# Gate and up projection on bare 4-bit values: two matmul passes, a PSUM bank for each scale group, scales applied as the banks are read

## The reference

```
h = layernorm(x) * (1 + ca) + sa;   x = x + ga * attention(h, W_Q, W_K, W_V, W_O)     # causal
h = layernorm(x) * (1 + cb) + sb;   x = x + gb * ffn(h)

ffn(x):
    w_gu   = LUT[nibbles of gate_up_packed] * gate_up_scales     # [2816, 512], 4 groups of 128 inputs
    w_down = LUT[nibbles of down_packed] * down_scales           # [512, 1408]
    gate, up = split(x @ w_gu.T)                                 # 1408 features each
    y = (silu(gate) * up) @ w_down.T
    return y / sqrt(mean(y * y) + 1e-6)
LUT = 0, 0.5, 1, 1.5, 2, 3, 4, 6 and their negatives
```

## Time and profile before

| | |
|---|---|
| median of 3 runs | 2338.56 us (2337.83 to 2340.6) |
| the profiled execution | 2341.84 us |
| span of its trace | 2339.8 us |
| TensorE matmul busy | 2235.7 us, 96% of the span |
| Vector engine, ScalarE, GpSimd busy | 52%, 42%, 27% |
| mean granted TensorE clock | 0.982 of full speed |

### The profile page before, as it was taken

One profiled execution on the slowest core, in us unless ns is written; L12 is line 12 of the kernel. 1 busy time (PEld: TensorE's weight loads), 2 busy tenths in 40 slices (PEclk: granted clock), 3 DMA queues, 4 the chain that ended last, 5 costly groups with the idle time before them and its releaser, 6 DMA issues. The chain is left out here.

```text
span 2339.8 us, 38212 instructions
## 1 busy us (share of the span) xinstructions
PE 2235.7 (96%) x12912; PEld 1909.9 (82%) x12912; DVE 1218.2 (52%) x2846; ACT 975.6 (42%) x1852; POOL 632.7 (27%) x470
## 2 busy tenths in 40 slices
PE   5899999999999999999999999999958888999899
PEld 3788888888888888888888888888847676888787
DVE  7364655656565565656555464555635553111465
ACT  4354544545455454545545454555523322111211
POOL 3435262543526254352601011010333330000000
PEclk8999999999999999999999999999979999999999
DMA  5111111101111110111100000000157763000121
GB/s 193 39 46 35 35 34 41 51 23 45 34 34 34 43 49 23 45 34 34 34 30 24 14 20 11 25 9 26 37 177 227 215 215 108 18 27 27 37 67 63
DMA packets 102320, 133.32 MB, mean 57 GB/s; under 512 B 9984, under 2 KB 68224, under 8 KB 102272
## 3 DMA queue, kind: packets, MB, share of 16 engines
q1 hardware_dynamic: 84128, 120.62, 16.2%
q10 hardware_dynamic: 18144, 12.06, 1.6%
HBM read 90.83 MB, written 33.95 MB: 53 GB/s over the span
## 5 line engine op out<-in xcount | busy, mean ns | idle before, releaser
L963 DVE TENSOR_SCALAR_CACHE_REDUCE probs<-ps_s 128x512 f32<-128x512 f32 (+3 forms) x640 | 371.2, 607 | 263.2 <-PE ps_t L830 116.8
L974 DVE TENSOR_TENSOR pT_lo<-ps_t,pT_hi 128x512 fp32r<-128x512 f32 (+3 forms) x640 | 368.6, 605 | 242.8 <-ACT pT_hi L895 241.6
L895 ACT ACTIVATE pT_hi<-ps_t 128x512 fp32r<-128x512 f32 (+3 forms) x640 | 318.7, 531 | 230.4 <-PE ps_t L830 229.6
L906 ACT ACTIVATE probs<-probs,rmin 128x128 f32<-128x128 f32 (+15 forms) x256 | 308.1, 1203 | 150.1 <-DVE rmin L967 124.9
L190 PE MATMUL ps_z<-pT_hi,v_hi 128*128 128x256 f32 (+1 forms) x1152 | 333.7, 290 | 0.3 <-issue 0.3
L190 PE MATMUL ps_p<-hT_hi,w_hi 128*128 128x512 f32 x768 | 320.7, 418 | 8.3 <-POOL halves L708 3.7
L191 PE MATMUL ps_z<-pT_lo,v_hi 128*128 128x256 f32 (+1 forms) x1152 | 324.8, 282 | 0.0
L192 PE MATMUL ps_z<-pT_hi,v_lo 128*128 128x256 f32 (+1 forms) x1152 | 324.7, 282 | 0.0
L830 PE MATMUL ps_t<-ident,probs 128*128 128x128 f32 x2176 | 309.6, 273 | 8.3 <-ACT probs L906 5.8
L192 PE MATMUL ps_p<-hT_hi,w_lo 128*128 128x512 f32 x768 | 303.5, 395 | 0.0
L191 PE MATMUL ps_p<-hT_lo,w_hi 128*128 128x512 f32 x768 | 301.6, 393 | 0.0
(11 more groups left out here) (146 smaller groups left out, 3685.7 us busy)
## 6 DMA issues: line engine op xcount, KB each, us to landing
scratch_zT<-z SPq DMA_DIRECT2D x256, 64.0 KB, 1.6
o_z<-scratch_zT SPq DMA_DIRECT2D x32, 512.0 KB, 4.6
o_scales<-scratch_recips SPq DMA_DIRECT2D x32, 512.0 KB, 5.7
w_raw<-in_w_qkv SPq DMA_DIRECT2D x16, 768.0 KB, 4.7
p_wmod<-in_w_mod SPq DMA_DIRECT2D x6, 1024.0 KB, 10.9
words<-in_gu_packed SPq DMA_DIRECT2D x44, 128.0 KB, 3.4
scratch_wgu<-deq_a SPq DMA_DIRECT2D x22, 256.0 KB, 2.0
g_wraw<-scratch_wgu SPq DMA_DIRECT2D x11, 512.0 KB, 3.5
```

What stands on the lines that cost most here:

```text
L895: nc.scalar.activation(pT[0][:, slot, i % 2, 0:w], ps_t[:, (chunks_before(i) + u) % 2, 0:w], ACT.Copy).then_inc(t_hi, 1)
L906: nc.scalar.activation(probs[:, i % 2, 0:w], probs[:, i % 2, 0:w], ACT.Exp, bias=rmin[:, i % 2:i % 2 + 1], scale=-1.0, accum_out=sums[:, i ...
L963: nc.vector.tensor_scalar(probs[:, i % 2, c * BT:c * BT + w], ps_s[:, at % NB, 0:w], 1.0, None, ALU.mult, ALU.min, accum_out=least).then_i ...
L974: nc.vector.tensor_tensor(pT[1][:, slot, i % 2, 0:w], ps_t[:, (chunks_before(i) + u) % 2, 0:w], pT[0][:, slot, i % 2, 0:w].bitcast(F32), A ...
```

## The change

The gate and up weights are no longer multiplied by their scales in the decoding, and no longer split. The scratch tensor `wgu` holds the bare 4-bit values as fp32r numbers. `gate_up` multiplies them by the high and by the low part of the activations, two passes. Since the scale is different for each chunk of 128 inputs, each of the four chunks gets a PSUM bank of its own. A step is one feature tile, one block of 512 tokens, and gate or up: 88 steps `j` with four banks each, on two sets of banks in turn. The banks are combined with the scale as a number for each partition:

- ScalarE reads banks 0 and 2 and multiplies by their scales (`first_of_pair`, new line 1344);
- the Vector engine reads banks 1 and 3, multiplies by their scales and adds ScalarE's result (`second_of_pair`, 1370), which gives two pairs;
- GpSimd adds the two pairs into `whole` (1396);
- ScalarE applies silu to the gate's `whole` (1352), and the Vector engine multiplies it by the up's `whole` into `mid` (`product`, 1379). Both read SBUF now.

The loops over the feature tiles are written out, without a loop instruction. SyncE loads the codes of tiles 0 and 1 in the output projection, and those of tile n once tile n-2 is done. The scales, 88 rows of 128, are loaded once, widened by ScalarE, transposed by TensorE and copied to SBUF in the output projection's tiles 1 and 2. `decode_piece` has eight instructions for a gate and up piece, one of them on a single column, and nine for a down piece; before it had nine. The 22 loads of gate and up scales in attention are gone.

```diff
 class GateUpWeights(NamedTuple):
-    raw: object
-    parts: object
+    codes: object
+    scales: object
     loaded: object
-    hi: object
-    lo: object
+    scales_ready: object
     def load(self, eng, hbm, n):
-        eng.dma_start(self.raw[:, :, :, :].rearrange("p c m n -> p (c m n)"),
-                      hbm["wgu"][bass.ds(n, 1), :, :].rearrange("a p n -> (a p) n")).then_inc(self.loaded, 16)
-    def make_hi(self, nc, act, n, m):
-        act.wait_ge(self.loaded, 16 * (n + 1))
-        nc.scalar.activation(self.parts[m][0][:, :, :], self.raw[:, :, m, :], ACT.Copy).then_inc(self.hi, 1)
-    def make_lo(self, nc, dve, n, m):
-        dve.wait_ge(self.hi, 2 * n + m + 1)
-        nc.vector.tensor_tensor(self.parts[m][1][:, :, :], self.raw[:, :, m, :],
-                                self.parts[m][0][:, :, :].bitcast(F32), ALU.subtract).then_inc(self.lo, 1)
+        eng.dma_start(self.codes[:, n % 2, :].bitcast(F32), hbm["wgu"][n]).then_inc(self.loaded[n % 2], 16)
+    def code(self, n, c, m):
+        return self.codes[:, n % 2, (2 * c + m) * P:(2 * c + m + 1) * P]
+    def scale(self, n, c, m):
+        at = 2 * (DC * n + c) + m
+        return self.scales[:, at:at + 1]
...
@@ attention, decoding on GpSimd @@
-                sp.dma_start(qscale[:, :], gu_scales[bass.ds(h, 1), k, :].to_broadcast([P, D])) \
-                  .then_inc(qscale_loaded, 16)
...
-            pool.wait_ge(qscale_loaded, 16 * (base + 1))
             wait_for(pool, deq_saved, 16 * base)
-            wait_for(pool, deq_step, made)
-            nc.gpsimd.tensor_tensor(deq_b[:, :], qscale[:, :], halves_wide, ALU.mult).then_inc(deq_step, 1)
-            nc.gpsimd.tensor_scalar(sign_f, words[:, :], -0.25, 1.0, ALU.mult, ALU.add).then_inc(deq_step, 1)
-            nc.gpsimd.tensor_scalar(deq_a[:, :], code[:, :], 4.0, -16.0, ALU.max, ALU.add).then_inc(deq_step, 1)
-            pool.wait_ge(deq_step, made + 3)
-            nc.gpsimd.tensor_tensor(sign_f, sign_f, deq_b[:, :], ALU.mult).then_inc(deq_step, 1)
-            nc.gpsimd.tensor_scalar(code_f, code[:, :], 1.0, None, ALU.mult).then_inc(deq_step, 1)
-            pool.wait_ge(deq_step, made + 5)
-            nc.gpsimd.tensor_tensor(deq_a[:, :], deq_a[:, :], code_f, ALU.add).then_inc(deq_step, 1)
-            nc.gpsimd.tensor_scalar(deq_b[:, :], code_f, 6.0, 2.0, ALU.max, ALU.mult).then_inc(deq_step, 1)
-            pool.wait_ge(deq_step, made + 7)
-            nc.gpsimd.tensor_tensor(deq_a[:, :], deq_a[:, :], deq_b[:, :], ALU.add).then_inc(deq_step, 1)
-            pool.wait_ge(deq_step, made + 8)
-            nc.gpsimd.tensor_tensor(deq_a[:, :], deq_a[:, :], sign_f, ALU.mult).then_inc(deq_step, 1)
+            wait_for(pool, deq_step, made[0])
+            then(nc.gpsimd.tensor_tensor(turn[:, :], zeros[:, 0:1], zeros[:, 0:1], ALU.add))
+            then(nc.gpsimd.tensor_scalar(sign_f, words[:, :], -0.125, 0.5, ALU.mult, ALU.add))
+            then(nc.gpsimd.tensor_scalar(deq_a[:, :], code[:, :], 4.0, -16.0, ALU.max, ALU.add))
+            then(nc.gpsimd.tensor_scalar(deq_b[:, :], code[:, :], 6.0, 2.0, ALU.max, ALU.mult))
+            pool.wait_ge(deq_step, made[0])
+            then(nc.gpsimd.tensor_tensor(deq_a[:, :], deq_a[:, :], deq_b[:, :], ALU.add))
+            if k == 2:
+                pool.wait_ge(qscale_loaded, 16 * (h + 1))
+                then(nc.gpsimd.tensor_tensor(sign_f, sign_f, qscale[:, :], ALU.mult))
+            then(nc.gpsimd.tensor_scalar(code_f, code[:, :], 1.0, None, ALU.mult))
+            pool.wait_ge(deq_step, made[0])
+            then(nc.gpsimd.tensor_tensor(deq_a[:, :], deq_a[:, :], code_f, ALU.add))
+            pool.wait_ge(deq_step, made[0])
+            then(nc.gpsimd.tensor_tensor(deq_a[:, :], deq_a[:, :], sign_f, ALU.mult))
...
@@ output_projection @@
-        gu.load(sp, hbm, 0)
+        sp.dma_start(s_half[:, :], gu_scales.rearrange("n k (c p) -> (n k c) p", p=P)).then_inc(s_loaded, 16)
+        for n in range(2):
+            gu.load(sp, hbm, n)
...
-            if isinstance(t, int) and t == 1:
-                for m in range(2):
-                    gu.make_lo(nc, dve, 0, m)
...
+            if isinstance(tile.t, int) and tile.t == 1:
+                act.wait_ge(s_loaded, 16)
+                nc.scalar.activation(s_rows[:, :], s_half[:, :], ACT.Copy).then_inc(s_wide, 1)
+            if isinstance(tile.t, int) and tile.t == 2:
+                act.wait_ge(s_turned, 1)
+                nc.scalar.activation(gu.scales[:, :], ps_scales[:, 0:2 * DC * NI], ACT.Copy) \
+                  .then_inc(gu.scales_ready, 1)
...
-            if isinstance(tile.t, int) and tile.t == 1:
-                for m in range(2):
-                    gu.make_hi(nc, act, 0, m)
...
+            if isinstance(t, int) and t == 1:
+                pe.wait_ge(s_wide, 1)
+                n = 2 * DC * NI
+                nc.tensor.transpose(ps_scales[:, 0:n], s_rows[:, :], ident[0:n, 0:n]).then_inc(s_turned, 1)
...
@@ gate_up @@
+    first_terms = sb("g_first", [P, 2, 2, BT], F32)
+    pairs = sb("g_pairs", [P, 2, 2, BT], F32)
+    whole = sb("g_whole", [P, 2, 2, BT], F32)
+    sg = sb("g_silu", [P, 2, BT], F32)
+    ps = ph.enter_context(nc.psum_tensor("g_ps", [P, 2, DC, BT], F32))
...
+    STEPS = [(n, b, m) for n in range(NI) for b in range(NB) for m in range(2)]
...
+        for n in range(2, NI):
+            sp.wait_ge(group_ready, DC * 2 * NB * (n - 1))
+            gu.load(sp, hbm, n)
+    @block.tensor
+    def _(pe):
+        for j, (n, b, m) in enumerate(STEPS):
+            if b == 0 and m == 0:
+                pe.wait_ge(gu.loaded[n % 2], 16 * (n // 2 + 1))
+            for c in range(DC):
+                if j >= 2:
+                    pe.wait_ge((first_ready, pair_ready)[c % 2], 2 * (j - 2) + c // 2 + 1)
+                w = gu.code(n, c, m)
+                hi, lo = [part[:, c, b * BT:(b + 1) * BT] for part in hT]
+                nc.tensor.matmul(ps[:, j % 2, c, :], w, hi, start=True, stop=False)
+                nc.tensor.matmul(ps[:, j % 2, c, :], w, lo, start=False, stop=True).then_inc(group_ready, 1)
...
+        def first_of_pair(j, e):
+            n, b, m = STEPS[j]
+            act.wait_ge(group_ready, DC * j + 2 * e + 1)
+            if j >= 2:
+                act.wait_ge(pair_ready, 2 * (j - 2) + e + 1)
+            nc.scalar.activation(first_terms[:, j % 2, e, :], ps[:, j % 2, 2 * e, :], ACT.Copy,
+                                 scale=gu.scale(n, 2 * e, m)).then_inc(first_ready, 1)
+        def silu(q):
+            act.wait_ge(whole_ready, 2 * q + 1)
+            if q >= 2:
+                act.wait_ge(mid_ready, q - 1)
+            nc.scalar.activation(sg[:, q % 2, :], whole[:, q % 2, 0, :], ACT.Silu).then_inc(silu_ready, 1)
+        act.wait_ge(gu.scales_ready, 1)
+        for j in range(len(STEPS)):
+            for e in range(2):
+                first_of_pair(j, e)
+            if j >= 2 and j % 2 == 0:
+                silu(j // 2 - 1)
+        silu(NI * NB - 1)
...
-                gu.make_lo(nc, dve, n + 1, 0)
-            for b in range(NB):
-                dve.wait_ge(up_ready, NB * n + b + 1)
-                dve.wait_ge(silu_ready, NB * n + b + 1)
-                dst = mid[:, bass.ds(n, 1), b * BT:(b + 1) * BT].rearrange("p a n -> p (a n)")
-                nc.vector.tensor_tensor(dst, sg[:, b, :], ps[1][:, b, :], ALU.mult).then_inc(mid_ready, 1)
-            if not last:
-                gu.make_lo(nc, dve, n + 1, 1)
...
+        def second_of_pair(j, e):
+            n, b, m = STEPS[j]
+            dve.wait_ge(group_ready, DC * j + 2 * e + 2)
+            dve.wait_ge(first_ready, 2 * j + e + 1)
+            if j >= 2:
+                dve.wait_ge(whole_ready, j - 1)
+            nc.vector.scalar_tensor_tensor(out=pairs[:, j % 2, e, :], in0=ps[:, j % 2, 2 * e + 1, :],
+                                           scalar=gu.scale(n, 2 * e + 1, m), in1=first_terms[:, j % 2, e, :],
+                                           op0=ALU.mult, op1=ALU.add).then_inc(pair_ready, 1)
+        def product(q):
+            n, b = divmod(q, NB)
+            dve.wait_ge(silu_ready, q + 1)
+            dve.wait_ge(whole_ready, 2 * q + 2)
+            nc.vector.tensor_tensor(mid[:, n, b * BT:(b + 1) * BT], sg[:, q % 2, :], whole[:, q % 2, 1, :], ALU.mult) \
+              .then_inc(mid_ready, 1)
+        dve.wait_ge(gu.scales_ready, 1)
+        for j in range(len(STEPS)):
+            for e in range(2):
+                second_of_pair(j, e)
+            if j >= 3 and j % 2:
+                product(j // 2 - 1)
+        product(NI * NB - 1)
+    @block.gpsimd
+    def _(pool):
+        for j in range(len(STEPS)):
+            q, m = divmod(j, 2)
+            pool.wait_ge(pair_ready, 2 * j + 2)
+            if q >= 2:
+                pool.wait_ge((silu_ready, mid_ready)[m], q - 1)
+            nc.gpsimd.tensor_tensor(whole[:, q % 2, m, :], pairs[:, j % 2, 0, :], pairs[:, j % 2, 1, :], ALU.add) \
+              .then_inc(whole_ready, 1)```

```

(50 more changed lines are left out.)

41 lines of the change are left out of this document (22 added, 19 removed).

## The result

The changed kernel takes 2264.07 us (median of 4 runs, 2262.45 to 2267.28), the kernel before 2338.49 (2337.83 to 2340.6): ratio 0.9678 [0.9661, 0.9694], 74.4 us less. The forecast was 2265 us in a range of 2258 to 2284. The total came out where it was put; two of its five terms did not, and they nearly cancelled. The profiled execution after took 2265.68 us, its span is 2263.9.

What follows compares the result with a forecast made beforehand. TensorE's matmuls were taken to bound gate_up. From the profiled 2341.84 us, -79.8 (matmuls) + 2.1 (pace) + 2.7 (stage end) + 1.5 (output projection) + 0 (attention) = -73.5 gave 2268.3; median-adjusted 2265 us, range 2258 to 2284.

Steps and rivals of the forecast that it cites:

- Matmuls: In gate_up, 1056 matmuls become 704; 352 fewer at 0.2267 us each give -79.8 us, start-up unchanged.
- Pace: In gate_up, matmuls slow somewhat beside busy engines and semaphore waits: 0 to +4.6 us, taken as +2.1.
- Readers: In gate_up, ScalarE, the Vector engine and GpSimd keep up with TensorE's 3.63 to 3.70 us per two steps.
- The limit of 3.24 us for two steps: In gate_up, a lagging Vector engine overlaps instruction starts: 4 x 0.66 + 0.60 us, so it catches up.
- rival 1: In gate_up, the Vector engine becomes the bound without overlap: 3.86 us per two steps, +8.1, 2273 us; chance 0.14.
- GpSimd beside the Vector engine: In gate_up, product and GpSimd addition exclude each other; product starts first, GpSimd loses 0.6 us per two steps, priced at nothing.
- rival 2: In gate_up's odd steps GpSimd starts first and the product waits 1.29 us: +43 us, 2308; chance 0.08.
- rival 3: In gate_up, the column scalar counts as second SBUF read, so GpSimd shuts out combinations: +114 us, 2379; chance 0.03.
- End of the stage: After gate_up's last matmul, combination, product, addition and last product take 3.3 us instead of 0.69, plus handovers: +2.7 us.
- Output projection: Two more transfers ahead of tile 1's loads, against ScalarE's dropped weight splits: +1.5 us, between -1 and +4.
- two short copies come in its place: In the output projection's tile 1, short copies replace ScalarE's weight splitting, which ran from 1764.63 to 1765.79.
- Attention: GpSimd saves some 2 us per gate and up piece and 22 small loads go: 0, between -1 and +1 us.

Runs made afterwards that it cites:

- one pass: Changed kernel without gate_up's second pass (low part of the activations left out, half the matmuls): 2247.16 us, ratio 0.9597; first to last matmul 144.56 us.

## Why the prediction was right, and where it was not

*Matmuls.* Right: -79.8 forecast, 80.4 less from first to last start, 0.7 of it from a start-up that is shorter.

*Pace.* "While other engines work, matmuls of the same size run somewhat slower" failed: +2.1 was put, and 0, its lower bound, came. The matmuls of `gate_up` start 0.2268 us apart beside engines busy 93, 87 and 82% of the time. Neither busy neighbours nor a semaphore wait ahead of every second matmul slows them. What makes the 0.2333 of the earlier trace rows is open.

*Readers.* Right. The limit of 3.24 us for two steps is measured at 3.27 (one pass), and rival 1, which had 3.86 for want of overlap, is refuted: five instructions whose records sum to 4 x 0.75 + 0.68 = 3.68 us are through in 3.27, with semaphores to wait for. ScalarE was within its bounds, 0.688 us a first term.

*GpSimd beside the Vector engine.* Right in its mechanism and in who wins. Products of 0.68 refute rival 2 here; where GpSimd was made to be first, in another place of the order, it cost 12 us and TensorE's waits. Combinations of 736 to 754 ns beside GpSimd at 82% refute rival 3: a column scalar from SBUF beside a PSUM operand does not make the instruction one that GpSimd shuts out. The Trainium skill (SBUF — State Buffer, Who interferes with whom) says that a Vector instruction with two SBUF inputs contends with a GpSimd instruction that reads SBUF. By this trace a column scalar beside one SBUF and one PSUM operand does not count as the second. The additions in odd steps took 1.68, not "near 1.9": 0.39 longer, not 0.6.

*End of the stage.* Right: +2.7 forecast, +2.9 measured. From the last combination on, the tail is the addition of 1.64 us and the product of 0.69 behind it:

```profile
2122.64 1.47 DVE L1370 SCALAR_TENSOR_TENSOR g_pairs<-g_ps,g_scales,g_first 128x512 f32<-128x512 f32 x2 [0.24 <-ACT g_first L1344]
2124.02 0.68 DVE L1379 TENSOR_TENSOR mid<-g_silu,g_whole 128x512 f32<-128x512 f32 x1
2124.18 1.64 POOL L1396 TENSOR_TENSOR g_whole<-g_pairs 128x512 f32<-128x512 f32 x1 [0.43 <-DVE g_pairs L1370]
2125.92 0.69 DVE L1379 TENSOR_TENSOR mid<-g_silu,g_whole 128x512 f32<-128x512 f32 x1 [1.22 <-POOL g_whole L1396]
```

*Output projection.* The step that failed is "two short copies come in its place". The copies were taken for short work and got no term of their own, and the prediction did not ask what stands ahead of the copy in ScalarE's queue (tile 1's square root, which waited 3.99 us for the variance) nor who waits for it (TensorE, 7.22 us). The term was to be about +8 rather than +1.5 (256.6 - 248.1 = 8.5 by the means over the traces), and the +8.15 between the profiled executions lies outside the bounds of -1 and +4. The transfers ahead of tile 1, which did have a price of 2.6 to 3.5 us, are not seen to cost it: tile 1 starts 2 us later, but no earlier with the second code load moved away. What delays it stays open.

*Attention.* The step that failed is "it waited 522.9 us for work there, and TensorE not for it". GpSimd waits in sum, but once in a head its save gates SyncE's next load, and that load gated the Vector engine: 1.08 us, 11 times, by which each such head was some 0.6 us longer. The row of that wait, 11.9 us, stood in the view of waits of the kernel before and was not read. The term is -6.8, outside -1 to +1.

So the mechanism of the large term and its size were right, with the rivals of `gate_up` refuted by runs. That the total fell within 1 us of the forecast is chance: between the profiled executions the terms are off by -6.8 (attention), -2.7 (pace and start-up), +6.7 (output projection) and +0.4 (the rest), -2.4 together.

## What to carry to other kernels

An engine that waits most of the time can still gate something: follow what its last instruction releases (here a save, and behind it in the same queue a load), and read the small waits that recur once per iteration: 1.08 us in each of 11 heads made the kernel some 7 us slower. A moved instruction is priced by its place in an in-order queue, by what stands ahead of it and who waits behind it, before its length. A change's total is checked stage by stage: a sum that fits can hide two errors of 7 us.
